# A quantised feed-forward and a recurrence, rebuilt as three blocks whose stages run interleaved, on one Trainium2 core

## The reference

```python
h = h + _L0_attn_ref(_layernorm(h), ...)
h = h + _L0_ffn_ref(_layernorm(h), ...)
h = h + _L1_attn_ref(_layernorm(h), ...)

def _act_fake_quant(x, clip_factor):
    scale = jax.nn.sigmoid(clip_factor) * jnp.max(jnp.abs(x)) / QMAX       # one scale for all of x
    return jnp.clip(_ste_round(x / scale), -QMAX - 1.0, QMAX) * scale
xq = _act_fake_quant(x, clip_x[0])
gate = einsum('bsh,ih->bsi', xq, _weight_fake_quant(w_gate))               # 704 inner features
up = einsum('bsh,ih->bsi', xq, _weight_fake_quant(w_up))                   # weights: a scale per row
h = _act_fake_quant(jax.nn.silu(gate) * up, clip_down[0])
return einsum('bsi,hi->bsh', h, _weight_fake_quant(w_down))

# _L1_attn_ref
x = inputs * rsqrt(mean(inputs * inputs, -1) + EPS) * norm_weight
probs = softmax(mean(x, axis=1) @ router_w.T + router_b)                   # per batch, 8 experts
W_hg = einsum('be,ekd->bkd', probs, w_hg);  W_out = einsum('be,eod->bod', probs, w_out)
hidden, gate = split(einsum('bsd,bkd->bsk', x, W_hg))
# a first-order recurrence over the 1024 positions, in logarithms
out = einsum('bsk,bok->bso', h, W_out);  return out + inputs
```

## Time and profile before

| | |
|---|---|
| median of three runs | 4348.81 us |
| profiled execution, its own time | 4352.46 us |
| its span, first to last instruction | 4350.7 us |
| mean granted TensorE clock | 0.963 of full speed |
| busy: DVE, ACT, POOL | 73%, 61%, 44% |
| attention ends (last DVE operation on its output) | 1049.0 us |
| first work of the local layers on TensorE | 1375.3 us |

### The profile page before, as it was taken

The page is one execution under the profiler, slowest core; times in us unless marked ns, Lnnn a source line. Parts: engine busy times, 40 slices in busy tenths (PEclk is TensorE's granted clock), DMA queues, the critical chain, the costliest instruction groups (busy, mean ns, idle before and its releaser), DMA issues. The chain is left out here.

```text
span 4350.7 us, 98162 instructions
## 1 busy us (share of the span) xinstructions
PE 4037.7 (93%) x33170; PEld 2814.9 (65%) x33172; DVE 3164.0 (73%) x5506; ACT 2640.2 (61%) x7021; POOL 1908.4 (44%) x1269
## 2 busy tenths in 40 slices
PE   6999979997426999999999999999999999999997
PEld 3666546664113677777777777777777777777776
DVE  4888448885865777777777777777777777777774
ACT  2677536774302666666666666666666666666664
POOL 1000000000002666666656666665666666566662
PEclk8999989999668999999999999999999999999999
DMA  6111141221022100111002100111002100111001
GB/s 154 40 44 44 23 114 44 55 55 32 0 69 96 23 20 19 50 45 27 20 19 61 39 20 21 49 45 27 20 19 60 40 19 21 49 47 25 20 19 49
DMA packets 102633, 178.80 MB, mean 41 GB/s; under 512 B 26756, under 2 KB 61472, under 8 KB 101792
## 3 DMA queue, kind: packets, MB, share of 16 engines
q1 hardware_dynamic: 101408, 170.87, 14.7%
q0 software_dynamic: 768, 2.10, 0.3%
HBM read 96.10 MB, written 23.07 MB: 27 GB/s over the span
## 5 line engine op out<-in xcount | busy, mean ns | idle before, releaser
L1855 POOL TENSOR_TENSOR swp<-raw,table 128x512 f32<-128x512 f32 x384 | 480.8, 1274 | 638.9 <-DVE ss L2266 638.8
L1017 DVE TENSOR_REDUCE maxima<-PS 128x1 f32<-128x512 f32 x1024 | 632.2, 680 | 123.8 <-PE PS L851 123.3
L1938 PE MATMUL PS<-wqk,xT 128*128 128x512 f32 x1536 | 687.7, 601 | 5.6 <-DMA wqk<-in_L_ffn_Wqkv 4.4
L1885 POOL TENSOR_TENSOR probs<-probs,prob_recip 128x512 f32<-128x512 f32 x384 | 476.4, 1260 | 430.4 <-DVE prob_recip L2324 430.4
L981 ACT ACTIVATE probs<-PS 128x512 f32<-128x512 f32 x1024 | 520.0, 603 | 155.2 <-PE PS L865 154.7
L2195 ACT ACTIVATE probs<-probs,neg 128x128 f32<-128x128 f32 x1536 | 595.9, 389 | 27.2 <-DVE neg L2318 25.7
L1865 POOL TENSOR_TENSOR rinv<-ssm,power 128x32 f32<-128x32 f32 x96 | 526.8, 5488 | 0.0
L1938 PEld LDWEIGHTS PS<-wqk,xT 128*128 128x128 f32 x1536 | 284.0, 190 | 336.8 <-issue 254.1
L2041 PE MATMUL PS<-xnT,w 128*128 128x128 f32 x3840 | 477.3, 276 | 0.4 <-DVE hidden L2384 0.4
L851 PE MATMUL PS<-k_stack,q_stack 112*128 112x512 f32 (+1 forms) x1024 | 430.8, 442 | 35.0 <-PEq L384 18.5
L2266 DVE TENSOR_REDUCE ss<-swp 128x16 f32<-128x1024 f32 x192 | 232.9, 1213 | 304.8 <-ACT swp L2146 304.8
...
## 6 DMA issues: line engine op xcount, KB each, us to landing
...
q_stack<-spin_qk SPq DMA_DIRECT2D x128, 80.0 KB
k_stack<-spin_qk SPq DMA_DIRECT2D x128, 80.0 KB
q_stack<-tok_qk SPq DMA_DIRECT2D x128, 64.0 KB
k_stack<-tok_qk SPq DMA_DIRECT2D x128, 64.0 KB
...
```

Of the source, the lines that this page charges most:

```text
L1017: dve.tensor_reduce(maxima[:, k // 2, k % 2:k % 2 + 1], SM(r, k), AX.X, ALU.max).then_inc(sm_maxed, 1)
L1855: pool.tensor_tensor(swp[:, w, :, a:a + LD // 2], raw[:, w, :, b:b + LD // 2], table[:, j % 2, 2 + w, a:a + LD // 2].rearrange("p (o d) -> ...
L1885: pool.tensor_tensor(view, view, psr[:, 4 * q:4 * q + 4].rearrange("p (h o) -> p h o", o=1) .to_broadcast([P, 4, P]), ALU.mult).then_inc(p ...
L1938: mm = pe.matmul(wide(kind, half, j), xT[:, k, at:at + P], rhs, start=(k == 0), stop=(k == DC - 1))
```

## The change

The row of blocks becomes three. Around them, pieces of work move into the second attention.

- The second attention takes four guests (`beside` in `attend`, `others` in `over_heads`): at its start POOL clears a padding, at step 5 SP issues the loads of the feed-forward's weights and POOL adds the output bias to c.H, and near the end ScalarE takes an exponential and DVE finds the scales of the weights and rounds them (`round`).
- `join_outputs` transposes and projects the attention's output pair by pair of tiles, adds it to h, takes the statistics and norms chunk by chunk, and finds the largest |x| with it, while ScalarE and TensorE finish the weights.
- `feed_forward` has two phases. In the first, x is clipped, rounded and transposed chunk by chunk, and gate, up, silu and product follow in the order of chunks; DVE takes the maximum over three pieces at once. In the second, eight pairs of tiles go through a pipeline: ScalarE scales the inner values and adds MAGIC, DVE clips them, **POOL** takes MAGIC away and writes bf16 (`round_h`), TensorE does the down projection, DVE scales it, POOL adds it to h, DVE takes statistics, POOL does the roots of both norms (the second from the variance), DVE norms, ScalarE scales again, TensorE transposes and sums for the mean, and the router follows.
- `recurrence` mixes the experts' w_hg unit by unit on DVE, so that a unit's matmuls begin when its own part is mixed; w_out is weighted on ScalarE and summed on POOL. The tail (output, addition, statistics, norm, store of h) goes chunk by chunk, and x + input is one addition, since POOL has added x to h before.
- Of the boundaries that clear semaphores, the one before `spin_projections` now stands behind it, and there is one less in all.

```diff
-def layernorm(c, src, dst, eps=EPS):
...
-def output_projection(c, context, w):
...
-def quantised_ffn(c, source):
...
-def quantise_activations(c, ctx, src, scratch, dst, clips, act_scale, which, part=None):
...
-            for i in range(n // piece):
-                at = slice(i * piece, (i + 1) * piece)
-                act.wait_ge(rounded, 2 * i + 2)
-                act.activation(dst[:, at], own[:, at], ACT.Copy, bias=-MAGIC).then_inc(taken, 1)
...
-def quantise_weights(c, ctx, source, gateT, downT, up_scale, out_scale, clips):
...
-def recurrence(c, source):
...
-def spill(c, src, dst, meanwhile):
...
+class QuantisedWeights:
...
+    def round(self, c, dve):
...
+        for w in range(2):
+            for j in range(IC):
+                dve.tensor_scalar(self.wide[:, w, j, :], self.wide[:, w, j, :], inv[:, w, j:j + 1], MAGIC, ALU.mult, ALU.add).then_inc(self.step, 1)
+        for m in range(DC):
+            dve.tensor_scalar(self.down[:, m, :], self.down[:, m, :], dsc[:, 1, m:m + 1], MAGIC, ALU.mult, ALU.add).then_inc(self.step, 1)
...
-        with nc.cleanup_on_exit():
-            loaded = [c.sem(f"stack_loaded{r}") for r in range(RING)]
-            spin_projections(c, V, qs, ks, second, loaded, context, w, s)
-            attend(c, V, qs, ks, second, loaded, context, HD + 4)
-            output_projection(c, context, w["next"])
+            spin_projections(c, V, qs, ks, second, spin_loaded, context, w, s, shared)
+        spin.close()
+        with nc.cleanup_on_exit():
+            with ExitStack() as weights:
+                m = QuantisedWeights(c, weights, shared)
+                attend(c, V, qs, ks, second, spin_loaded, context, HD + 4, {
+                    "pool": {0: lambda pool: m.clear(c, pool), RING - 1: lambda pool: m.add_bias(c, pool, w["next"]["bo"])},
+                    "sp": {RING - 1: lambda sp: m.load(c, sp)},
+                    "act": {ITERS + 1: lambda act: m.exponent(c, act)},
+                    "dve": {ITERS + 2: lambda dve: m.round(c, dve)}})
+                join_outputs(c, context, w["next"]["wo"], m)
...
+def join_outputs(c, context, wo, m):
...
+                for ch in range(CHUNKS):
+                    at = slice(4 * ch, 4 * ch + 4)
+                    pool.wait_ge(moments_ready, 4 * ch + 4)
+                    pool.tensor_scalar(shifted[:, at], moments[:, at, 1], EPS, None, ALU.add).then_inc(shift_done, 1)
+                    pool.wait_ge(shift_done, ch + 1)
+                    pool.tensor_tensor(rstd[:, at], shifted[:, at], power[:, at], ALU.pow).then_inc(rstd_ready, 1)
+                pool.wait_ge(peak_ready, 1)
+                pool.partition_all_reduce(peak[:, 1:2], peak[:, 0:1], P, bass.bass_isa.ReduceOp.max).then_inc(all_peak, 1)
...
+                def norm(ch):
+                    dve.wait_ge(rstd_ready, ch + 1)
+                    for t in range(4 * ch, 4 * ch + 4):
+                        dve.tensor_scalar(c.X[:, t, :], c.H[:, t, :], moments[:, t, 0:1], rstd[:, t:t + 1],
+                                          ALU.subtract, ALU.mult).then_inc(normed, 1)
+                    dve.wait_ge(normed, 4 * ch + 4)
+                    dve.tensor_reduce(parts[:, ch:ch + 1], c.X[:, 4 * ch:4 * ch + 4, :].rearrange("p t d -> p (t d)"), AX.X, ALU.max,
+                                      apply_absolute_value=True).then_inc(part_done, 1)
...
+                for ch in range(CHUNKS):
+                    add_output(2 * ch)
+                    add_output(2 * ch + 1)
+                    count(ch)
+                    if ch:
+                        norm(ch - 1)
+                norm(CHUNKS - 1)
+                dve.wait_ge(part_done, CHUNKS)
+                dve.tensor_reduce(peak[:, 0:1], parts[:, :], AX.X, ALU.max).then_inc(peak_ready, 1)
...
+def feed_forward(c, m, x):
...
+                pool.memset(hT[64:P, IC - 1, :], 0.0).then_inc(cleared, 1)
+                pool.wait_ge(cleared, 1)
+                pool.memset(power[:, :], -0.5).then_inc(cleared, 1)
+                pool.memset(ones[:, :], 1.0).then_inc(cleared, 1)
+                pool.wait_ge(cleared, 3)
+                pool.wait_ge(peak_ready, 1)
+                pool.partition_all_reduce(peak[:, 1:2], peak[:, 0:1], P, bass.bass_isa.ReduceOp.max).then_inc(all_peak, 1)
+                def add_output(g):
+                    pool.wait_ge(out_scaled, g + 1)
+                    at = slice(PAIR * g, PAIR * g + PAIR)
+                    pool.tensor_tensor(c.H[:, at, :], c.H[:, at, :], scaled_out[:, g % 2, :, :], ALU.add).then_inc(ffn_added, 1)
+                def deviations(g):
+                    at = slice(PAIR * g, PAIR * g + PAIR)
+                    pool.wait_ge(moments_ready, PAIR * g + PAIR)
+                    pool.tensor_scalar(small[:, 0, at], moments[:, at, 1], EPS, None, ALU.add).then_inc(pool_step, 1)
+                    pool.wait_ge(pool_step, 4 * g + 1)
+                    pool.tensor_tensor(rstd[:, at], small[:, 0, at], power[:, at], ALU.pow).then_inc(rstd_ready, 1)
...
+                    pool.tensor_tensor(rr[:, at], small[:, 3, at], power[:, at], ALU.pow).then_inc(rr_ready, 1)
+                def join(g):
+                    at = slice(PAIR * g, PAIR * g + PAIR)
+                    pool.wait_ge(normed, PAIR * g + PAIR)
+                    pool.tensor_tensor(c.H[:, at, :], c.H[:, at, :], c.X[:, at, :], ALU.add).then_inc(h_joined, 1)
+                def round_h(g):
+                    pool.wait_ge(h_clipped, g + 1)
+                    wait(pool, down_done, g - 1)
+                    pool.tensor_scalar(hq[:, g % 2, :, :], hT[:, :, PAIR * g * P:PAIR * (g + 1) * P], MAGIC, None, ALU.subtract).then_inc(h_rounded, 1)
+                for g in range(PAIRS + 2):
+                    if g < PAIRS:
+                        round_h(g)
+                    if 1 <= g <= PAIRS:
+                        add_output(g - 1)
+                        deviations(g - 1)
+                    if g >= 2:
+                        join(g - 2)
...
+                def to_integers(g):
+                    view = hT[:, :, PAIR * g * P:PAIR * (g + 1) * P]
+                    act.activation(view, view, ACT.Copy, scale=m.act_scale[:, 1, 1:2], bias=MAGIC).then_inc(h_magic, 1)
...
+                def clip_h(g):
+                    view = hT[:, :, PAIR * g * P:PAIR * (g + 1) * P]
+                    dve.wait_ge(h_magic, g + 1)
+                    dve.tensor_scalar(view, view, MAGIC + QMAX, MAGIC - QMAX - 1.0, ALU.min, ALU.max).then_inc(h_clipped, 1)
...
+                for g in range(PAIRS + 3):
+                    if g < PAIRS:
+                        clip_h(g)
+                    if 1 <= g <= PAIRS:
+                        count(g - 1)
+                    if g < PAIRS:
+                        scale_output(g)
+                    if 1 <= g <= PAIRS:
+                        norm(g - 1)
+                    if g >= 3:
+                        take_normed(g - 3)
...
+def recurrence(c, x, spilled):
...
+                for b in range(BATCH):
+                    for e in range(1, E):
+                        n = (E - 1) * b + e - 1
+                        pool.wait_ge(multiplied, E * b + e + 1)
+                        if n:
+                            pool.wait_ge(summed, n)
+                        pool.tensor_tensor(x.mixed_out[:, b, :, :], x.mixed_out[:, b, :, :], product[:, n % 2, :, :], ALU.add).then_inc(summed, 1)
...
+                def weigh_output(b, e):
...
+                    act.activation(dst, x.wout[:, e, :, :], ACT.Copy, scale=x.share[:, b, e:e + 1]).then_inc(multiplied, 1)
...
+                for e in range(E):
+                    weigh_output(0, e)
+                sigmoids(0)
+                for e in range(E // 2):
+                    weigh_output(1, e)
+                sigmoids(1)
+                for e in range(E // 2, E):
+                    weigh_output(1, e)
+                sigmoids(2)
+                sigmoids(3)
...
+                    for e in range(E):
...
+                            if e == 0:
+                                dve.tensor_scalar(dst, src, by, None, ALU.mult).then_inc(mixed_in, 1)
+                            else:
+                                dve.wait_ge(mixed_in, at - DC + 1)
+                                dve.scalar_tensor_tensor(out=dst, in0=src, scalar=by, in1=dst, op0=ALU.mult, op1=ALU.add).then_inc(mixed_in, 1)
...
+                mix(0)
+                mix(1)
+                mix(2)
+                scan(0)
+                mix(3)
+                scan(1)
+                scan(2)
+                scan(3)
...
-            attentions(c)
+            shared = c.sb(first, "shared", [P, 6 * CH])
+            m = attentions(c, shared)
             with nc.cleanup_on_exit():
-                quantised_ffn(c, lambda: layernorm(c, c.H, c.X))
-                recurrence(c, lambda: layernorm(c, c.H, c.X))
-            with nc.cleanup_on_exit():
-                spill(c, c.H, spilled, lambda: layernorm(c, c.H, c.X))
```

(4 more changed lines are left out.)

1070 lines of the change are left out of this document (617 added, 453 removed).

## The result

| | before | changed |
|---|---|---|
| median of four runs each | 4348.7 us (4347.1 to 4349.6) | 4321.8 us (4314.6 to 4326.6) |
| profiled execution, its span | 4352.46 us, 4350.7 | 4326.64 us, 4324.7 |
| ratio, 95% interval | | 0.9937 (0.992 to 0.9954) |
| granted clock of the profiled execution | 0.963 | 0.962 |

The changed kernel is faster, but by less than half of the forecast, and it lies above the range of 4255 to 4306. Its runs also differ from each other by 12 us where those of before differ by 2.5, and the profiled one is the slowest of the four.

The account below looks back on a forecast made before the run. No engine was taken to bound the region, DVE being nearest; its blocks ran one after another. 1.4 + 29.3 + 47.0 + 92.6 + 79.0 = 249.3 against 318.3 us, -69.0, gave 4280 us, bounds 4255 to 4306.

Parts of the forecast that it names:

- End of attention, +1.4: Second attention's end: weight rounding, 12.0 us on DVE, delays the last inversions, so attention ends at 1050.4, not 1049.0.
- Join, 29.3: Join block: 72.0 to 29.3 us, from a 3.4 us chain, 23.0 of DVE work and 2.9 at the end.
- exchange: End of join: POOL swaps its code for the all-reduce in 5.7 us, of which 1.4 us stay open.
- Gate, 47.0: Gate and up block: 50.3 to 47.0 us, from 10.9 start, 33.5 of DVE work and 2.6 for peak and scale.
- TensorE's 24 units of 1.04 us lie beside it: Gate and up block: TensorE's matmuls run beside DVE's work, three banks deep, and add nothing to the sum.
- Down stage, 92.6: Down, norms, router: 91.4 to 92.6 us, POOL becoming the bound with 9.7 us per pair of tiles.
- exclusion: Certain DVE operations and POOL's run one at a time; in the down stage norm (0.65) and clip_h (0.75) lengthen POOL's cycle.
- second rival: Down stage: POOL heavier than priced, round_h at 3.8 or each pair's whole chain in turn, cycle 12 to 13; 4302, chance 0.17.
- Recurrence, 79: Recurrence block: 104.6 to 79 us, by less DVE addition and mixing and fewer boundaries between blocks.
- first rival: POOL and DVE pass each other and lose nothing: recurrence -14, down stage -7, 4259 us; chance 0.2.
- Local layers, 0: Six local layers after 1367 us: instruction streams kept, so no change was priced.
- Slow POOL path: Down stage: round_h falls on a slow POOL path, 6370 us in all, deciding from 6.9 ns an element; chance 0.03.

Follow-up runs that it names:

- e1: The changed kernel with round_h moved from POOL back to ScalarE; 4294.1 us.
- e3: The changed kernel with 35 more already-met semaphore waits on TensorE ahead of the local layers, shifting only its loop's place in the code; 4303.7 us.
- e4: The changed kernel with 100 more already-met semaphore waits on TensorE ahead of the first down projection, shifting only its loop's place; 4299.3 us.
- e7: The changed kernel with w_out's mixture on DVE instead of ScalarE and POOL, and 39 more semaphore instructions on TensorE; 4297.1 us.
- e5: The changed kernel plus single POOL and DVE operations behind its end, alone and together; POOL's scalar subtraction of 1536 elements took 4.1 us.

## Why the prediction was wrong, step by step

Two steps carry it: round_h priced at 1.9 us where it takes 4.1, and the local layers put at nothing where they lost 15.2 us. The rest is smaller.

- **End of attention, +1.4: it cost nothing.** Without the low-clock spin stage, attention ended at 1045.1 to 1047.3 (e1, e3, e4, e7), no later than in before. From the write of `context` ahead of the rounding to the last one 12.05 us pass in both kernels (1036.65 to 1048.70; 1042.68 to 1054.73). The rounding took 9.9 us, not 12.0, its twelve scalings 3.24 and not 4.6, since they start 0.27 apart. It made the inversion of the earlier trace rows 2.2 us late, and the one behind it had 3.3 us of waiting to give. My step had taken it that the last one hangs on the last but one. The guests (seven DMAs, eight additions) cost nothing.
- **Join, 29.3: 31.3.** Right in kind. The exchange and the open wait were as named, 2.59 us where I had 1.4, and two waits of 1.47 for TensorE's projections were missing.
- **Gate, 47.0: 52.9.** The start was right (11.5 us to the first product, forecast 10.9), clip_x beside the memset took 2.30 us as forecast. The step that failed is "TensorE's 24 units of 1.04 us lie beside it": behind the first product DVE waited 6.9 us for silu, for which the sum had nothing. The clock of 0.76 is the likely reason, as profiles with 0.80 to 0.85 have 49 to 52 us, but that is argued and not shown.
- **Down stage, 92.6: 104.2.** The mechanism was right: POOL the bound, wait 1.1, exclusion (the second addition took 1.46 or more where it met DVE). The step that failed is the price of round_h, 1.9 by a copy's rate with a two-input rate as the upper end. It is 4.1, 2.2 us more in each pair, while the rest of the cycle came to 7.2 and not 7.8. From the first round_h to the last 74.65 us pass, forecast 63.6: +11.0. The first one started 6.7 us into the stage and not 4.8, since the code's exchange took 7.12: +1.9. From the last one's start to the shares it was 1.3 shorter than forecast. The cycle of 11.3 us lies between the forecast's 9.7 and the second rival's 12 to 13. Of that rival the price came true (it had 3.8 us), not the chain of a whole pair. I gave it 0.17 because I held a one-input operation to be cheaper than a two-input one.
- **The Trainium skill's rates.** GPSIMD Engine Reference, sections 3.1 and 4.1 (about line rate, the 1.3 us of my estimate), are off by a factor of three for a subtraction here, and near for a copy (0.95 ns an element here; 1.03 cycles at 1.2 GHz, as section 3.1 has it, give an estimate of 0.86). Its section 2.1 has about 6 us for newly loaded code: the 5.9 us ahead of the all-reduce agree, the 7.1 us on the way back are more.
- **Recurrence, 79: 82.7.** The first mixture took 13.3 us (forecast 14), DVE and POOL alternating. With the same code there the block took 80.3 us in e3 and 83.1 in e4; why it varies, and why it came out 1 to 4 us above the forecast stays open. The first rival (they pass each other, 4259) falls with e5 and e7. The row that spoke for it, the power of the earlier trace rows, was rightly read, and holds for that operation.
- **Local layers, 0: +15.2.** The step that failed is a term put at nothing, by the words "keep their instruction streams, so I only price what lies between". The stream was the same, its place in the code was not, and at that place TensorE stood for 3.1 to 3.7 us behind each of four branches and then ran at the lower clock: 17.5 us. With that cost taken away (e3, e4) the changed kernel takes 4299 to 4304, inside the range and at the second rival's 4302. My text did name layers whose own length differs by more than 3 us as what would prove it wrong, but gave no mechanism and no chance to it.
- **Slow POOL path (0.03).** It came half true: POOL's scalar arithmetic is a slower path than its copy, 2.54 ns an element, far from the 6.9 from which it decides.
